# A gated attention and feed-forward block on one core: another order of its engines, and loads issued from ScalarE

## The chip, the cores and the metric

One Trainium2 chip, one of its cores. The metric is the device time of one execution in microseconds (us), lower is better. TensorE (PE) multiplies, VectorE (DVE), ScalarE (ACT) and GpSimd (POOL) compute elementwise, SyncE (SP) issues DMAs. TensorE's clock has two levels, 1.2 and 2.4 GHz; the profile gives the granted share of full speed.

## The reference

For 32 x 256 tokens of D = 256 features. The attention's mask lets each query see one key with the same position (and there are as many queries as keys), so attention is a projection by the value and output weights; its gate is tanh(g_x). Then a quantised feed-forward part with H = 1024:

```python
x = x + tanh(g_xattn[0]) * (context @ Wv @ Wout + bout)
h = layernorm(layernorm(x), ln1_g, ln1_b)
h = bitlinear(h, w1, b1)
h = gelu(h)
h = layernorm(h, ln2_g, ln2_b)
x = x + tanh(g_ffn[0]) * bitlinear(h, w2, b2)
```

where `bitlinear` rounds a token's features to 8 bits by its largest magnitude, and the weights to -1, 0, 1 by their mean magnitude, multiplies, and scales back.

## The kernel before

The 8192 tokens are cut into S = 16 sets of 128 partitions x T = 4 tiles. Each engine has a program of its own, written as `body(i)` for i from -3 to S + 1, and waits for the others on semaphores; the order of work is the order in which the bodies are written. A body deals with several sets at once:

- TensorE (L934): transposes the context of set i + 3 and 4 (`turn_context`, L937, into `bank_q`), multiplies by the joint weight `wvo` (`attention`, L1017), turns the rows of split statistics (`turn_rows`, L1053), adds bias and mean terms with small matmuls (`correction`, L1065, for y of set i - 1; `shift_first`, L1075, for h1 of set i + 1), makes the hidden layer of set i (`hidden`, L1084, alternately in `slot_a` and `slot_b`) and the second product of sets i - 2 (tiles 0, 1) and i - 3 (tiles 2, 3) (`second_product`, L1104, `second_bias`, L1115).
- ScalarE: quantises h1 of set i to `q1` (L540), copies contexts (L510) and rows (L556), quantises y of set i - 2 to `q2` (L549), and for each of the four tiles of set i a gelu (L566) and a square for the variance (L576).
- VectorE: residual and statistics of set i + 2, for set i - 1 four times `row` (y plus correction, L771) and `row_max` (L778), h1's shift and maximum (L757, L765), final results (`final`, L815), and the small operations of `scales` (L783) that give the quantisers' factors for set i + 1 (first layer) and i - 1 (second layer).
- POOL: gains (`gain`, L391, 128x1024 each; `gain_first`, L382), mean and variance (`norm_first`, L398, `variance`, L408), `root` (L373, a power of -0.5 for the two layers at once), `deviations` (L417) and five steps of `split` (L424), which cut six statistics into three bf16 parts for the rows.
- SP: loads x and context, issues DMA transposes of q1 and q2 (`turn_first`, L229; `turn_second`, L239) and stores. It issues in order: what stands behind a waiting load waits too.

Ahead of the bodies the kernel multiplies Wv by Wout (`turn_values`, `combine`), and quantises w1 and w2 in the first bodies. Bodies S and S + 1 finish the last sets.

```python
            for i in range(2, S):
                if live(i - 3):
                    turn_second(i - 3, 3)
                if live(i):
                    turn_first(i)
                if live(i - 2):
                    turn_second(i - 2, 0)
                if live(i + 4):
                    load_x(i + 4)
```

## Time and profile before

| what | value |
|---|---|
| median of 3 runs | 356.12 us (355.98 to 356.35) |
| profiled execution, its time | 356.32 us |
| its span, first to last instruction | 354.5 us |
| busy PE, DVE, ACT, POOL | 296.9, 294.9, 277.2, 265.2 us |
| mean granted TensorE clock | 0.957 |
| HBM traffic | 21.79 MB read, 8.41 MB written |

Busy time counts what an engine computes, not its semaphore or DMA instructions. A timeline row gives start, duration, engine, source line and tiles; the bracket at its end is idle time before it and what ended that. A name such as `q` or `rows` leaves out buffer numbers, so `q` is q1 at L544 and q2 at L553.

### The profile page before, as it was taken

The numbers are of one execution on the slowest core, as the hardware profiler recorded it, in microseconds if no ns is written. First come the engines' busy times: TensorE is split into PE (matmuls) and PEld (weight loads), VectorE is DVE, ScalarE is ACT, GpSimd is POOL, SyncE is SP. The second block draws the span as 40 slices with busy tenths as digits, with TensorE's granted clock in tenths as the row PEclk, the third lists the DMA queues.
The fourth block names the chain that finished last, engine by engine and source line by source line (L and its number), as shares of the span: only waits on it lengthen the run. The fifth ranks groups of instructions, "written<-read, shape, count | busy, mean of one in ns | idle before, by whom it ended". The sixth has DMA issues, their size and how long they took to land. (4 is left out here: it accounts for less than half of the span.)

```text
span 354.5 us, 5862 instructions
## 1 busy us (share of the span) xinstructions
PE 296.9 (84%) x1680; PEld 191.7 (54%) x1704; DVE 294.9 (83%) x521; ACT 277.2 (78%) x444; POOL 265.2 (75%) x298
## 2 busy tenths in 40 slices
PE   5998887889898979898989899989998849394566
PEld 4867463537475646465656565655655424242344
DVE  0268898989999999999999999989999948666582
ACT  2155696898989899998989898989898977779340
POOL 4045789997989888989898989898898986738410
PEclk9999999989999999999999999999999978978598
DMA  7956513364858685768666767595555445361457
GB/s 220 324 188 252 151 61 89 118 150 119 189 131 182 111 204 138 170 157 145 182 154 159 160 164 152 165 150 150 112 97 106 104 95 114 74 133 38 82 115 213
DMA packets 98634, 51.57 MB, mean 145 GB/s; under 512 B 87097, under 2 KB 89588, under 8 KB 98602
## 3 DMA queue, kind: packets, MB, share of 16 engines
q1 hardware_dynamic: 97706, 51.15, 59.5%
q8 instruction: 14, 0.23, 0.3%
q10 hardware_dynamic: 896, 0.04, 0.2%
q14 instruction: 18, 0.15, 0.1%
HBM read 21.79 MB, written 8.41 MB: 85 GB/s over the span
## 5 line engine op out<-in xcount | busy, mean ns | idle before, releaser
L395 POOL TENSOR_TENSOR y<-u,g_bc 128x1024 f32<-128x1024 f32 x64 | 151.0, 2368 | 15.3 <-ACT u L572 14.3
L776 DVE TENSOR_TENSOR y<-y,slot_c 128x1024 f32<-128x1024 f32 x64 | 77.7, 1214 | 23.3 <-PE slot_c L1070 23.3
L780 DVE TENSOR_REDUCE amax<-y 128x1 f32<-128x1024 f32 x64 | 78.0, 1218 | 1.8
L553 ACT ACTIVATE q<-y,scale 128x1024 f16<-128x1024 f32 x64 | 70.0, 1144 | 8.2 <-DVE scale L811 8.2
L580 ACT ACTIVATE junk<-u,usum 128x1024 bf16<-128x1024 f32 x64 | 73.7, 1151 | 2.0
L1112 PE MATMUL bank_f<-w2T,q2T 128*128 128x256 f16 x448 | 60.7, 281 | 7.4 <-DVE res L823 5.5
L1112 PEld LDWEIGHTS bank_f<-w2T,q2T 128*128 128x128 f16 x448 | 44.6, 101 | 23.5 <-DVE res L823 6.1
L1028 PE MATMUL slot_a<-wvo,ctxT 128*128 128x256 f32 x208 | 53.4, 386 | 1.0 <-ACT ctxT L515 1.0
L1070 PE MATMUL slot_c<-ln_rows,rows 128*128 128x512 bf16 x119 | 38.1, 397 | 16.6 <-ACT rows L563 7.2
L572 ACT ACTIVATE u<-slot_a,d 128x1024 f32<-128x1024 f32 x32 | 35.5, 1109 | 10.8 <-PE slot_a L1099 9.3
L1028 PEld LDWEIGHTS slot_a<-wvo,ctxT 128*128 128x128 f32 x208 | 36.3, 190 | 11.1 <-ACT ctxT L515 3.6
L1099 PE MATMUL slot_a<-w1T,q1T 128*128 128x512 f16 x128 | 40.5, 400 | 0.5 <-issue 0.2
L544 ACT ACTIVATE q<-h,scale 128x256 f16<-128x256 f32 x64 | 27.4, 500 | 13.8 <-DVE scale L811 13.8
L1099 PE MATMUL slot_b<-w1T,q1T 128*128 128x512 f16 x128 | 38.1, 380 | 0.0
L386 POOL TENSOR_TENSOR h<-x,g_bc 128x1024 f32<-128x1024 f32 x15 | 35.5, 2368 | 0.0
L572 ACT ACTIVATE u<-slot_b,d 128x1024 f32<-128x1024 f32 x32 | 35.1, 1097 | 0.0
L378 POOL TENSOR_TENSOR rstd<-var,half_neg 128x8 f32<-128x8 f32 x18 | 30.2, 1675 | 2.4
L1070 PEld LDWEIGHTS slot_c<-ln_rows,rows 128*128 128x128 bf16 x128 | 10.3, 99 | 33.9 <-issue 17.3
L823 DVE SCALAR_TENSOR_TENSOR res<-bank_f,d,x 128x256 f32<-128x256 f32 x56 | 24.4, 478 | 3.4 <-PE bank_f L1118 3.4
L745 DVE BATCH_NORM_STATS2 bn<-x 128x6 f32<-128x256 f32 x64 | 24.1, 418 | 1.0
L1096 PE MATMUL slot_b<-b_rows,rows 128*128 128x512 bf16 x64 | 24.5, 383 | 0.0
L515 ACT COPY ctxT<-bank_q 128x512 f32<-128x512 f32 x32 | 18.3, 572 | 6.2 <-PE bank_q L948 6.2
(136 smaller groups left out, 430.9 us busy)
## 6 DMA issues: line engine op xcount, KB each, us to landing
c_in<-in_ctx SPq DMA_DIRECT2D x16, 512.0 KB, 4.2
x_in<-in_x SPq DMA_DIRECT2D x16, 512.0 KB, 4.1
out<-res SPq DMA_DIRECT2D x31, 256.0 KB, 2.5
y<-in_L_ffn_w SPq DMA_DIRECT2D x2, 1024.0 KB, 9.0
u<-in_L_xattn_Wkv SPq DMA_DIRECT2D x2, 512.0 KB, 6.2
u<-in_L_xattn_Wout SPq DMA_DIRECT2D x2, 512.0 KB, 7.4
q2T<-q SPq DMA_TRANSPOSE x64, 3.3
g_bc<-in_L_ffn_ln_g SPq DMA_DIRECT2D x1, 512.0 KB, 5.5
```

The lines of the kernel that those rows point to most:

```text
L378: nc.gpsimd.tensor_tensor(rstd[:, j % 2, :, :], var[:, :, :], half_neg[:, :, :], ALU.pow) \
L386: nc.gpsimd.tensor_tensor(h1[:, :, :], x1[:, k % SETS, :, :], g1_bc[:, :].unsqueeze(1).to_broadcast([P, T, D]), ALU.mult) \
L395: nc.gpsimd.tensor_tensor(y[:, k % 3, t, :], u[:, t, :], g2_bc[:, :], ALU.mult).then_inc(gain2_done, 1)
L553: nc.scalar.activation(q2[:, t, :], y[:, k % 3, t, :], ACT.Copy, scale=scale[:, (k + 1) % 2, 1, t:t + 1]).then_inc(q2_done, 1)
L572: nc.scalar.activation(u[:, t, :], (slot_a, slot_b)[t % 2][:, :], ACT.Gelu, scale=d12[:, (i - 1) % 3, 0, t:t + 1], accum_out=usum[:, t:t + ...
L580: nc.scalar.activation(junk[:, t % 2, :], u[:, t, :], ACT.Square, scale=-float(H), bias=usum[:, t:t + 1], accum_out=usq[:, t:t + 1]) \
L776: nc.vector.tensor_tensor(line, line, slot_c[:, :], ALU.add).then_inc(y_done, 1)
L780: nc.vector.tensor_reduce(amax[:, 1, t:t + 1], y[:, k % 3, t, :], AX.X, ALU.max, apply_absolute_value=True).then_inc(amax2_done, 1)
L1028: nc.tensor.matmul(acc, ctxT[:, b * P:(b + 1) * P], wvo[:, j, :], start=(j == 0), stop=False)
L1070: terms = nc.tensor.matmul(slot_c[:, 512 * n:512 * (n + 1)], rows[:, (k + 1) % 2, t // 2, :], ln2_rows[:, t % 2, 512 * n:512 * (n + 1)], s ...
L1099: product = nc.tensor.matmul(slot[:, half], q1T[:, t * KD + k, :], w1T[:, k, half], start=False, stop=(k == KD - 1))
L1112: nc.tensor.matmul(product_bank(k, t), q2T[:, t, j, :], w2T[:, j, :], start=(j == 0), stop=False)
```

## The change

It rewrites the order on every engine and a few operations:

- From body 2 on the loads of x (set i + 4) and context (set i + 5) are issued by ScalarE, behind the second square and behind the fourth gelu; SP has only transposes and stores in its loop. SP's earlier loads are reordered.
- POOL's root is split: `root_first` (128x4) right after `norm_first`, `root_second` (128x4) where `root` stood; `variance` computes the mean row before it waits for the squares.
- `scales` has five operations instead of six (the lower limit joins others), `scale_weights` fewer, and `deq_inv` is gone.
- TensorE's body turns context earlier and makes second product 0 after the hidden layer, product 1 ahead of both attention halves. For bodies 13 to 15 `keep_warm` adds ten 128x512 matmuls of no use at the end, for 14 and 15 eight ahead of `turn_rows`.
- The end has one more body. POOL handles the last set's statistics in two pairs of tiles (`pair_root`, `pair_deviations`, a smaller `split` at i == S), and rows are turned three times.
- At the start the value weights come and are turned in four parts, with VectorE and ScalarE copying in turn; TensorE has 22 instead of 14 warm-up matmuls that wait for a memset of VectorE only; weight sums, clamps, copies and the first context turns change places.

```diff
@@ @block.sync: weight loads in four parts, order of the first loads, loads out of the loop @@
-            for n in range(2):
-                cols = slice(512 * n, 512 * (n + 1))
+            for n in range(4):
+                cols = slice(256 * n, 256 * (n + 1))
...
             for i in range(2, S):
                 if live(i - 3):
                     turn_second(i - 3, 3)
                 if live(i):
                     turn_first(i)
+                if live(i - 3):
+                    store(i - 3, 1)
                 if live(i - 2):
                     turn_second(i - 2, 0)
-                if live(i + 4):
-                    load_x(i + 4)
-                if live(i - 2):
                     turn_second(i - 2, 1)
-                if live(i - 3):
-                    store(i - 3, 1)
-                if live(i + 5):
-                    load_context(i + 5)
                 if live(i - 2):
                     turn_second(i - 2, 2)
...
@@ @block.gpsimd: the root in two parts, tiles 0 and 1 of the last set ahead @@
-                def root(j):
+                def root_first(k):
 
-                    wait(pool, var1_done, min(j + 2, S))
+                    wait(pool, var1_done, k + 1)
+                    wait(pool, scales_ready, scales_after(k - 3))
+                    nc.gpsimd.tensor_tensor(rstd[:, (k - 1) % 2, 0, :], var[:, 0, :],
+                                            half_neg[:, 0, :], ALU.pow).then_inc(root1_done, 1)
+
+                def root_second(j):
+
                     wait(pool, var2_done, j)
                     wait(pool, scales_ready, scales_after(j - 2))
-                    nc.gpsimd.tensor_tensor(rstd[:, j % 2, :, :], var[:, :, :], half_neg[:, :, :],
-                                            ALU.pow) \
+                    nc.gpsimd.tensor_tensor(rstd[:, j % 2, 1, :], var[:, 1, :], half_neg[:, 1, :],
+                                            ALU.pow).then_inc(rstd_done, 1)
...
                 def variance(k):
 
+                    wait(pool, gelu_done, T * k + T)
+                    wait(pool, split_steps, split_count(i))
+                    nc.gpsimd.tensor_scalar(stat[:, 2, :], usum[:, :], -1.0 / H, None, ALU.mult)
                     wait(pool, square_done, T * k + T)
                     wait(pool, std_done, i + 2)
-                    wait(pool, split_steps, split_count(i))
-                    nc.gpsimd.tensor_scalar(stat[:, 2, :], usum[:, :], -1.0 / H, None, ALU.mult)
...
+                if i == S - 1:
+                    gain(S - 2, 3)
+                    gain(S - 1, 0)
+                    gain(S - 1, 1)
+                    pair_root(0)
+                    return
+                if i == S:
+                    pair_root(1)
+                    return
+                if i == S + 1:
+                    gain(S - 1, 2)
+                    gain(S - 1, 3)
+                    return
...
@@ @block.scalar: body(i) @@
                     square(0)
                     gelu(1)
                     square(1)
+                if live(i + 4) and i > 1:
+                    load_x(i + 4)
+                if live(i):
                     gelu(2)
                     square(2)
                     gelu(3)
+                if live(i + 5) and i > 1:
+                    load_context(i + 5)
+                if live(i):
                     square(3)
...
@@ @block.vector: scales @@
-                    nc.vector.tensor_tensor(amax_g[one], amax[one], power, ALU.mult) \
-                        .then_inc(scale_steps, 1)
+                    nc.vector.scalar_tensor_tensor(
+                        out=amax_g[one], in0=amax[one], scalar=1.0 / STEP, in1=power,
+                        op0=ALU.mult, op1=ALU.mult).then_inc(scale_steps, 1)
                     wait(dve, scale_steps, base + 1)
-                    nc.vector.tensor_scalar(amax_g[one], amax_g[one], QEPS, None, ALU.max) \
-                        .then_inc(scale_steps, 1)
-                    wait(dve, scale_steps, base + 2)
                     nc.vector.reciprocal(amax_inv[one], amax_g[one]).then_inc(scale_steps, 1)
...
@@ @block.tensor: warm-up, dummies, order of a body @@
-            for n in range(14):
-                nc.tensor.matmul(slot_c[:, 0:T * ROWS], ones_b[:, :], zeros, start=True, stop=True)
...
+            pe.wait_ge(zeros_ready, 1)
+            for n in range(22):
+                nc.tensor.matmul(slot_c[:, 0:D], junk[:, 0, 0:P], junk[:, 0, P:P + D],
+                                 start=True, stop=True)
+            pe.wait_ge(consts, 13)
...
+                def keep_warm(n, first=False):
+
+                    wait(pe, gelu_done, T * (i - 1) + 3 if first else T * min(i, S - 1) + 3)
+                    for _ in range(n):
+                        nc.tensor.matmul(slot_a[:, 512:1024], ident_b[:, :], b1_rows[:, 0, 0:512],
+                                         start=True, stop=True)
...
                 if i == S:
+                    second_product(S - 3, 2)
                     turn_rows()
+                    second_bias(S - 3, 2)
                     correction(S - 1, 0)
                     correction(S - 1, 1)
...
                 if i == S + 1:
                     turn_rows()
+                    correction(S - 1, 2)
+                    correction(S - 1, 3)
...
+                if i > S - 3:
+                    keep_warm(8, True)
                 if i <= S + 1:
                     turn_rows()
...
                 if live(i + 3):
                     attention(i + 3, 1)
+                else:
+                    keep_warm(10)
```

TensorE in a middle set, behind the hidden layer's last tile, before (L948 turns context, L1080 shifts h1, L1028 and L1032 are attention, L1112 and L1118 the second product):

```order
L948 MATMUL bank_q<-ident_f,c_in 128x128 x4
L1080 MATMUL slot_c<-ln1_rows,rows 128x512 x2
L1028 MATMUL slot_a<-wvo,ctxT 128x256 x2
L1032 MATMUL slot_a<-bout_rows,ones_b 128x256
L1028 MATMUL slot_a<-wvo,ctxT 128x256 x2
L1032 MATMUL slot_a<-bout_rows,ones_b 128x256
L1112 MATMUL bank_f<-w2T,q2T 128x256 x8
L1118 MATMUL bank_f<-b2_rows,rows 128x256
```

and after the change (L1039 turns context, L1178 shifts h1, L1123 and L1127 are attention, L1213 and L1220 the second product):

```order
L1213 MATMUL bank_f<-w2T,q2T 128x256 x8
L1220 MATMUL bank_f<-b2_rows,rows 128x256
L1178 MATMUL slot_c<-ln1_rows,rows 128x512 x2
L1213 MATMUL bank_f<-w2T,q2T 128x256 x8
L1220 MATMUL bank_f<-b2_rows,rows 128x256
L1123 MATMUL slot_a<-wvo,ctxT 128x256 x2
L1127 MATMUL slot_a<-bout_rows,ones_b 128x256
```

The second context turn went from here to a place ahead of hidden tile 2, in exchange for second product 0, and product 1 moved ahead of attention.

ScalarE in a middle set, gelus and squares, before:

```order
L572 ACTIVATE u,usum<-slot_b,d12 128x1024
L580 ACTIVATE junk,usq<-u,usum 128x1024
L572 ACTIVATE u,usum<-slot_a,d12 128x1024
L580 ACTIVATE junk,usq<-u,usum 128x1024
L572 ACTIVATE u,usum<-slot_b,d12 128x1024
L580 ACTIVATE junk,usq<-u,usum 128x1024
L515 COPY ctxT<-bank_q 128x512
```

and after the change:

```order
L644 ACTIVATE u,usum<-slot_b,d12 128x1024
L652 ACTIVATE junk,usq<-u,usum 128x1024
L608 DMA x_in<-in_x 128x1024
L644 ACTIVATE u,usum<-slot_a,d12 128x1024
L652 ACTIVATE junk,usq<-u,usum 128x1024
L644 ACTIVATE u,usum<-slot_b,d12 128x1024
L603 DMA c_in<-in_ctx_1024 128x1024
L652 ACTIVATE junk,usq<-u,usum 128x1024
L577 COPY ctxT<-bank_q 128x512
```

Two DMA issues now stand between the activations.

POOL at the end, from the gains of the last set, before:

```order
L395 TENSOR_TENSOR y<-u,g2_bc 128x1024 x4
L413 TENSOR_SCALAR stat<-usum 128x4
L414 TENSOR_SCALAR var<-usq 128x4
L378 TENSOR_TENSOR rstd<-var,half_neg 128x8
L421 TENSOR_TENSOR stat<-var,rstd 128x2x4
```

and after the change:

```order
L428 TENSOR_TENSOR y<-u,g2_bc 128x1024 x3
L399 TENSOR_SCALAR stat<-usum 128x2
L400 TENSOR_SCALAR var<-usq 128x2
L404 TENSOR_TENSOR rstd<-var,half_neg 128x2
L412 TENSOR_TENSOR stat<-var,rstd 128x2
L474 CAST parts<-stat 128x2x2x3
```

Tiles 0 and 1 get their statistics and root behind the second gain of the last set; gains 2 and 3 stand behind the second pair.

## Rows read from the trace of the kernel before

**Rows 1.** Busy by stage: start:end, us, PE, PEld, DVE, ACT, POOL busy, PEclk, DMA, GB/s

```profile
0.00:57.56 57.56, 46.94 (x253) 34.65 (x256) 35.04 (x81) 27.12 (x45) 30.94 (x59) 1.00 0.61 198
57.56:274.81 217.25, 197.76 (x1145) 127.35 (x1163) 206.93 (x357) 198.71 (x323) 190.20 (x193) 0.99 0.64 146
274.81:295.34 20.53, 14.52 (x72) 7.51 (x72) 14.91 (x21) 15.83 (x27) 16.59 (x17) 0.83 0.53 118
295.34:315.72 20.38, 14.61 (x71) 7.54 (x72) 14.21 (x20) 15.72 (x26) 13.03 (x13) 0.83 0.42 92
315.72:354.50 38.78, 23.11 (x143) 14.65 (x142) 23.84 (x44) 19.80 (x27) 14.41 (x18) 0.82 0.47 111
```

**Rows 2.** ScalarE timeline, middle set: start us, us, engine line, op, tiles, [idle before]

```profile
163.12 3.23 ACT L553 ACTIVATE q<-y,scale 128x1024 f16<-128x1024 f32 x3
166.28 1.12 ACT L572 ACTIVATE u<-slot_a,d 128x1024 f32<-128x1024 f32 x1
...
171.23 1.12 ACT L572 ACTIVATE u<-slot_a,d 128x1024 f32<-128x1024 f32 x1
...
176.00 0.57 ACT L515 COPY ctxT<-bank_q 128x512 f32<-128x512 f32 x1
...
178.47 1.71 ACT L544 ACTIVATE q<-h,scale 128x256 f16<-128x256 f32 x4 [0.86 <-DVE scale L811]
```

**Rows 3.** VectorE timeline, w1's sum in the head, then a middle set

```profile
17.57 2.29 DVE L681 TENSOR_REDUCE wsum<-y 128x1 f32<-128x2048 f32 x1 [5.31 <-DMA y<-in_L_ffn_w]
...
163.92 1.22 DVE L776 TENSOR_TENSOR y<-y,slot_c 128x1024 f32<-128x1024 f32 x1 [0.21 <-PE slot_c L1070]
...
166.97 1.21 DVE L776 TENSOR_TENSOR y<-y,slot_c 128x1024 f32<-128x1024 f32 x1
...
176.76 0.88 DVE L823 SCALAR_TENSOR_TENSOR res<-bank_f,d,x 128x256 f32<-128x256 f32 x2 [0.18 <-PE bank_f L1118]
...
177.74 0.17 DVE L797 TENSOR_SCALAR amax_g<-amax_g 128x8 f32<-128x8 f32 x1
...
181.94 1.22 DVE L776 TENSOR_TENSOR y<-y,slot_c 128x1024 f32<-128x1024 f32 x1 [0.21 <-PE slot_c L1070]
```

**Rows 4.** TensorE timeline, middle set, from correction 2 to the turn

```profile
168.33 0.59 PE L1070 MATMUL slot_c<-ln_rows,rows 128*128 128x512 bf16 x2 [0.36 <-DVE y L776]
168.76 1.04 PE L1112 MATMUL bank_f<-w2T,q2T 128*128 128x256 f16 x8
...
179.10 1.04 PE L1112 MATMUL bank_f<-w2T,q2T 128*128 128x256 f16 x8
...
180.55 0.28 PE L1059 MATMUL slot_c<-ident_b,parts 128*128 128x128 bf16 x2 [0.30 <-POOL parts L437]
```

**Rows 5.** POOL timeline behind the last square, middle set

```profile
176.17 0.22 POOL L413 TENSOR_SCALAR stat<-usum 128x4 f32<-128x4 f32 x1 [1.21 <-ACT junk L580]
...
176.79 1.67 POOL L378 TENSOR_TENSOR rstd<-var,half_neg 128x8 f32<-128x8 f32 x1
178.53 0.20 POOL L421 TENSOR_TENSOR stat<-var,rstd 128x8 f32<-128x8 f32 x1
```

**Rows 6.** Loads by source line, ns min/median/max; then landing of q2T's transposes

```profile
L222 SPq DMA_DIRECT2D c_in<-in_ctx x16: 328/335/812, 3.6 to 227.5; - x16
...
L227 SPq DMA_DIRECT2D x_in<-in_x x16: 327/570/1224, 4.0 to 238.1; - x16
...
DMA to landing us min/median/max: 3.0/3.3/6.1
```

**Rows 7.** TensorE timeline, sets 14 and 15: turns, corrections, the last products

```profile
289.10 0.39 PE L1059 MATMUL slot_c<-ident_b,parts 128*128 128x128 bf16 x2 [1.96 <-POOL parts L437]
289.96 1.03 PE L1070 MATMUL slot_c<-ln_rows,rows 128*128 128x512 bf16 x2 [0.47 <-ACT rows L563]
...
329.77 0.40 PE L1059 MATMUL slot_c<-ident_b,parts 128*128 128x128 bf16 x2 [6.67 <-POOL parts L437]
...
345.40 1.14 PE L1112 MATMUL slot_a<-w2T,q2T 128*128 128x256 f16 x8 [3.32 <-DMA q2T<-q]
```

More of the change, by code:

```diff
@@ L781, in row_max, with scales @@
                                             apply_absolute_value=True).then_inc(amax2_done, 1)
-                def scales(kinds=slice(0, 2), those=slice(0, T)):
+                def scales(kinds=slice(0, 2), those=slice(0, T), turn=0):
                     shape = [P, kinds.stop - kinds.start, those.stop - those.start]
-                    base = 3 * (i + 1 + (those.start > 0))
+                    base = 2 * (i + 1 + turn)
                     one = (slice(None), kinds, those)
@@ L791, in scales @@
                     wait(dve, amax2_done, T * (i - 1) + those.stop)
-                    wait(dve, rstd_done, i + 2)
-                    wait(dve, split_steps, split_count(i))
-                    nc.vector.tensor_tensor(amax_g[one], amax[one], power, ALU.mult) \
-                        .then_inc(scale_steps, 1)
+                    wait(dve, root1_done, min(i + 2, S))
+                    wait(dve, rstd_done, i + (those.stop > 2 and i == S))
+                    wait(dve, split_steps, split_count(i + (i == S)))
@@ L815, in final @@
+                    nc.vector.scalar_tensor_tensor(
+                        out=scale[:, i % 2, kinds, those], in0=amax_inv[one], scalar=STEP / QEPS, in1=power,
+                        op0=ALU.min, op1=ALU.mult).then_inc(scales_ready, 1)
                 def final(k, t):
-                    if k == S - 1:
-                        wait(dve, ffn_done, T * k + (t + 1 if t > 1 else 2))
+                    if k == S - 2:
+                        wait(dve, ffn_done, T * k + T)
+                    elif k == S - 1:
+                        wait(dve, ffn_done, T * k + t + 1)
@@ L915, in body @@
                     row_max(i - 1, 3)
-                if i == S:
-                    scales(slice(1, 2), slice(2, 4))
                 if live(i + 1):
```

344 lines of the change are left out of this document (205 added, 139 removed).

## The prediction, made before the changed kernel ran

> **What bounds the kernel now.** I cut the span at the first gelu of sets 0+1, 13, 14 and 15 and read each stretch in the busy times by stage [rows 1]. Sets 1 to 13 take 217.25 us for 12 periods, 18.10 each; VectorE is busy 206.93 of it, ScalarE 198.71, TensorE 197.76, POOL 190.20. Nothing idles for long, so a ring of engines sets the pace. Sets 13 and 14, with less work on TensorE and VectorE, take 20.53 and 20.38, and the last stretch 38.78; there TensorE's granted clock is 0.83, 0.83 and 0.82, so part of each runs at 1.2 GHz instead of 2.4.
>
> The timelines of one middle set show the ring. ScalarE starts q1 at 178.47 after waiting 0.86 for VectorE's scales [rows 2]. VectorE starts the first y row of a set at 163.92 and again at 181.94, a period of 18.02, after waiting only 0.21 for TensorE [rows 3]. TensorE waits 0.36 for y before a correction and 0.30 for POOL before it turns the rows [rows 4]. POOL waits 1.21 for the last square, then runs statistics, a `pow` of 1.67, deviations and five split steps [rows 5]. The ring is: scales at 160.4 (a period before 178.47), ScalarE to the end of the last square at 176.0, POOL to 180.55, turn, copy and correction to 181.94, VectorE until its scales at 196.45 (a period after 178.4). That is 36.0 for two periods, almost without slack: 18.0.
>
> **The change in the middle sets.** (a) POOL behind the square: one 0.22 statistic with its gap moves ahead of the wait (-0.29), and `pow` is made for 4 elements there, the other 4 earlier in the set. No row shows a `pow` of 4: it lies between the 0.20 of a plain 8-element operation and the 1.67 of 8 [rows 5]. I take the middle, 0.93, since an 8-element `pow` costs so much more than plain work on 8 that it seems to go with elements. Chain -0.29 -0.74 = -1.03. POOL's own work becomes at most 18.02 -1.21 -1.67 +2x0.93 +0.1 (a gap) = 17.1: not a bound.
> (b) Scales: five operations instead of six; the removed one lasts 0.17, 0.20 with its gap. VectorE also waits 0.18 for the second product, which now comes earlier. Its own work is 18.02 -0.21 -0.18 -0.20 = 17.43 [rows 3].
> (c) TensorE's order: nothing is added or lost in a middle set. From the first y row to the end of the second: 166.97 + 1.21 - 163.92 = 4.26 [rows 3]. From there to correction 2, 0.15; from 168.33 through the unchanged quantity of work to the turn, less its wait (180.55 - 0.30), 11.92; turn, copy, correction and hand-over to VectorE, 180.55 to 181.94, 1.39 [rows 3, 4]. Sum 17.72. **This one-period ring, VectorE to TensorE and back, is what is late next.** The ring (a) falls from 36.0 by 1.03, 0.38 and 0.18 (gelus 0 and 1 with squares take 171.23 - 166.28 = 4.95, gelus 2 and 3 take 4.77: gelu 2 waits for its product [rows 2], which now comes before the second product) to 34.4, or 17.2 a period, below it.
> (d) Loads from ScalarE: 10 of x behind square 1 and 9 of context behind gelu 3. SP's issues of the same loads take 0.34 and 0.57 in the median, 0.81 and 1.22 at most [rows 6]. If ScalarE's queue runs ahead of its arithmetic they cost 0; if it stands still, 0.91 a set, at most 2.03. The nearest row is SP's and says nothing on overlap; I take 0, because both stand behind an activation of 1.1 us that is already running. The cover is exactly that activation. Queued behind are the remaining gelus, the copy of ctxT and the attention that needs it. That ring is ScalarE q2 3.23, four gelus and squares 9.54, copy 0.57 [rows 2], TensorE's last transposes, attention and product until its turn 3.65 (from 176.6, where the copy ends, to 180.25, the same work in either order), turn and copy of rows 0.6: 17.6. It has 0.1 to spare; whatever issue costs beyond that lengthens each of 10 periods. On SP, where a load now waits for nobody, transposes are never queued behind a load's wait, which removes part of the occasional long period. They need 3.0 to 6.1 to land (median 3.3) [rows 6]. The loads have a whole period to land.
> The middle thus goes from 217.25 to 12 x 17.72 = 212.6: **-4.6**.
> The DMA side has a contrary rule. Trainium skill, DMA: Bandwidth & Descriptors, "Issuing engines are not separate DMA queues": requests from any engine run on the same 16 DMA engines, and another issuer saves only its sequencer's time. By it transposes meet the same traffic and about two periods could stay 0.5 longer, 1.0 more in all; the landing spread fits it, but no row has loads from ScalarE.
>
> **Head.** Weights come in halves, VectorE joins in the copies, warm-up starts without POOL, but w1 still arrives at 17.57 [rows 3]. Attention 0 may be 1.0 to 2 earlier but VectorE first sums w1 for 2.29, so what remains is about 0.7: the weights' sum no longer stands in front of hidden 0. The shortened POOL chain then meets set 1, limited by the copies of ctxT. I take **-1.2** for everything up to set 1's gelu at 57.56; between 0 and -2.3.
>
> **Sets 14 and 15.** Now TensorE turns at 289.10 after waiting 1.96 for POOL, the two corrections behind it last 1.03 against 0.59 in the middle, and the next gelu starts at 295.34 [rows 1, 4, 7]. Dummy matmuls (`keep_warm`) fill the waits: 10 at the end of a set, 8 before the turn. At 0.43 for two 128x512 [rows 4] they last 2.15 and 1.72. Counted from a set's first gelu, final results let the product end at 12.2, eight dummies end at 13.95, POOL would be ready at 13.05, so the turn is 0.9 late for them; then rows, three q2 of 1.08 and gelu at 17.85. Two sets: 35.7 against 40.91, **-5.2**. ScalarE is the end there, so TensorE's speed alone buys nothing more.
>
> **Tail.** Root, split and turn for tiles 0 and 1 of set 15 go ahead of its last gelus. Before, the turn came 329.77 - 315.72 = 14.05 behind the first gelu. Now POOL has those rows at about 9.2, but TensorE still has both products, ten dummies and one more product, to 11.2: the turn is 2.9 earlier, the first y row 3.3 earlier. The second half turns at 16.5, behind y row 1. Two more y rows with maxima, scales at 24.85, five splits, the third turn at 26.8 where the last four products began at 29.68 (345.40) [rows 7]. They still start cold after a 4 us gap, as they do now after 3.32. Their cost of about 5.4, and a last transpose that lands at 30.4, put the end at 35.4 in place of 38.78: **-3.4**.
>
> **Sum.** 354.5 -1.2 -4.6 -5.2 -3.4 = 340.1 span. The profiled execution took 356.32, 1.82 more than its span, and lies 0.2 above the median of 356.12. 340.1 + 1.82 - 0.2 = **341.7 us**.
>
> **Rivals.**
> A, `pow` has a fixed price, near 1.67 for 4 elements. For: every one of the 18 rows has 8 elements. Then POOL carries up to 15.2 + 3.34 = 18.5 a period, and 12 x 0.8 = 9, with 2 more in the last sets: 353. Decides from about 1.3 upwards. Against: plain POOL work scales. Chance 0.10.
> B, ScalarE stands still for SP's median times, 0.91 a set: 0.8 x 10 = 8: 349.7. Chance 0.14.
> C, dummies do not hold the clock. Eight then last 3.4, the turn is at 15.6, and correction, product and hidden run at 1.2 GHz: 21.8 a set instead of 17.85, +8: 349.7. For: TensorE is mostly idle there. Chance 0.08. Trainium skill, TensorE: Matmul & The Clock Gate, "What's actually happening": the array is throttled by default and activity releases it, which gives 341.7 if the dummies count and 349.7 if they do not. The granted clocks of rows 1 agree with the first half; no row here has dummies between waits.
> D, **slower**: the loads stop ScalarE for their long times, 0.81 + 1.22 = 2.03 a set. 17.6 + 2.03 = 19.6 against 17.72, +19 over ten periods: 360.7. Slower begins at about 1.6 a set. For: SP's own rows reach it. Against: medians are under half. Chance 0.03.
> E, the change does more: TensorE's gaps close until VectorE's 17.43 is the bound, and the tail's products stay warm: -3.5 and -1.5: 336.7. Chance 0.10.
> The forecast itself, 339 to 345: 0.55.
>
> **How the numbers follow.** 336.5 to 350 takes in the forecast, B, C and E and leaves out A, D and their combinations. A measurement tells 0.2% from nothing, 0.7 us. Only D and combinations of A, B and C reach 355.4: faster 0.95, same 0.02, slower 0.03.
>
> **What would show it.** Right: q1 to q1 at 17.7 in the middle with a VectorE wait of about 0.3 for TensorE at the first y row; `pow` near 0.9; no gap ahead of gelu 2; 17.9 between gelus 13, 14 and 15 at clock above 0.95; first y row of set 15 12.7 behind its first gelu. Wrong: periods of 18.4 with POOL never waiting for the square (A), gaps of 0.3 to 1.2 behind the loads on ScalarE (B, D), corrections of 1.03 in sets 14 and 15 (C).

## The result, and the profile after

The changed kernel takes 344.59 us (median of 4 executions, 343.29 to 346.18) beside 356.24 (355.98 to 356.75) for the kernel before on the same chip: ratio 0.967, 95% interval 0.963 to 0.972. 341.7 was forecast, with 336.5 to 350. The profiled execution took 343.99 us, with a span of 342.0. Three executions among the experiments below were slow ones (e5's profiled one with 778.87 us, one of e6 with 452.92, one of e9 with 346.75): the ratios leave them out, the medians of the table don't. The busy times and the clock of the profiled execution:

```profile
PE 299.9 (88%) x1735; PEld 192.6 (56%) x1760; DVE 292.4 (86%) x501; ACT 276.0 (81%) x446; POOL 269.3 (79%) x322
...
PEclk9999999999999999999999999999999999999989
```

Busy by stage, cut at the same gelus as [rows 1]: start:end, us, PE, PEld, DVE, ACT, POOL busy, PEclk, DMA, GB/s:

```profile
0.00:54.44 54.44, 47.99 (x261) 35.41 (x264) 34.78 (x78) 27.13 (x47) 29.97 (x61) 1.00 0.61 204
54.44:271.85 217.41, 195.94 (x1144) 125.32 (x1162) 205.55 (x344) 197.53 (x322) 195.12 (x206) 1.00 0.62 146
271.85:289.37 17.52, 15.88 (x90) 8.53 (x91) 13.78 (x20) 15.59 (x25) 15.29 (x16) 1.00 0.49 106
289.37:307.06 17.69, 15.95 (x91) 8.42 (x91) 13.94 (x20) 15.58 (x27) 13.10 (x14) 1.00 0.56 105
307.06:342.00 34.94, 24.13 (x154) 14.97 (x154) 24.39 (x43) 20.13 (x29) 15.80 (x27) 0.93 0.65 144
```

Against [rows 1]: head -3.12, sets 1 to 13 **+0.16**, the next two sets -5.70, the end -3.84; together -12.50. All of the gain is at the two ends of the kernel. In the middle nothing is left of the 4.6 us forecast.

Yet the middle does have the period that was forecast. VectorE's first y rows of sets 8 and 9:

```profile
178.24 1.22 DVE L860 TENSOR_TENSOR y<-y,slot_c 128x1024 f32<-128x1024 f32 x1 [0.21 <-PE slot_c L1167]
...
195.85 1.22 DVE L860 TENSOR_TENSOR y<-y,slot_c 128x1024 f32<-128x1024 f32 x1 [0.21 <-PE slot_c L1167]
```

That is 17.61, of which 0.21 is a wait: VectorE is full with 17.40 of work. In [rows 3] the period of 18.02 held waits of 0.21 and 0.18 and no other idle time, so VectorE had 17.63 of work and was as full as this in the kernel before. But from first gelu to first gelu the 12 periods are 17.93, 17.24, 17.91, **19.63**, 17.95, 17.96, 17.51, 17.61, **19.15**, 18.07, 17.98 and 18.47. TensorE's waits from 60 to 270 us name what fills the long ones (line and tile that waited, releaser: us in total, times, longest):

```profile
PE bank_f L1213 <- DMA q2T<-q: 5.7, 8, 2.0
```

In the kernel before, the same wait has two rows of 1.6 and 1.4 us. The worst place, in the period of 19.63: TensorE's second product of tile 1 waits, and the attention behind it is late for VectorE.

```profile
117.14 1.03 PE L1213 MATMUL bank_f<-w2T,q2T 128*128 128x256 f16 x8 [1.95 <-DMA q2T<-q]
```

```profile
118.32 0.88 DVE L909 SCALAR_TENSOR_TENSOR res<-bank_f,d,x 128x256 f32<-128x256 f32 x2 [0.55 <-PE bank_f L1220]
120.27 0.75 DVE L818 SCALAR_TENSOR_TENSOR x<-slot_a,tg,x_in 128x512 f32<-128x512 f32 x1 [0.48 <-PE slot_a L1127]
122.66 0.75 DVE L818 SCALAR_TENSOR_TENSOR x<-slot_a,tg,x_in 128x512 f32<-128x512 f32 x1 [0.85 <-PE slot_a L1127]
```

SP's queue at that place (L254 is the store, L248 the transpose of q2), then the loads from ScalarE's queue in the same microseconds:

```profile
108.26 0.33 SPq L254 DMA_DIRECT2D out<-res  x1
108.70 4.60 SPq L248 DMA_TRANSPOSE q2T<-q  x3
```

```profile
111.14 0.33 ACTq L608 DMA_DIRECT2D x_in<-in_x  x1
...
113.82 0.34 ACTq L603 DMA_DIRECT2D c_in<-in_ctx  x1
```

ScalarE had finished q2 of tile 0 by about 105.3 (its three q2 start at 104.09 and end at 107.32), but SP passes the store at 108.6, since that store waits for the fourth final result. Then three transposes go out back to back, and 1 MB of loads joins them. Two things are thus to be suspected: the loads, and that store.

In the last sets TensorE's dummies (L1228), turn and correction, where [rows 7] had a wait of 1.96 and a correction of 1.03:

```profile
283.93 1.89 PE L1228 MATMUL slot_a<-b_rows,ident_b 128*128 128x512 bf16 x8
285.66 0.28 PE L1155 MATMUL slot_c<-ident_b,parts 128*128 128x128 bf16 x2
286.40 0.61 PE L1167 MATMUL slot_c<-ln_rows,rows 128*128 128x512 bf16 x2 [0.46 <-ACT rows L635]
...
333.57 0.28 PE L1155 MATMUL slot_c<-ident_b,parts 128*128 128x128 bf16 x2 [0.84 <-POOL parts L474]
```

### The profile page after: what moved, and what is told of

It reads as the page before. It is cut to its first block, busy times and chain, and to the rows that moved or that the text cites. A ratio compares the mean times of both kernels' runs of the same rounds, so it can differ in the third digit from the quotient of the medians.

```text
span 342.0 us, 6023 instructions
## 1 busy us (share of the span) xinstructions
PE 299.9 (88%) x1735; PEld 192.6 (56%) x1760; DVE 292.4 (86%) x501; ACT 276.0 (81%) x446; POOL 269.3 (79%) x322
## 4 chain that ended last, share of the span: by engine, by line
DVE 29%; PE 22%; issue 14%; DMA 13%; ACT 4%; POOL 2%; SPq 2%; DVEq 0%; ACTq 0%; POOLq 0%
DVE y L860 14%; DMA q2T<-q 13%; DVE amax L864 7%; PE bank_f L1213 6%; PE slot_a L1123 5%; DVE res L909 5%; DVE h L845 3%; PE slot_c L1167 2%; PE slot_a L1228 2%; ACT u L644 1%; PE bank_q L1039 1%; ACT q L625 1%; ACT rows L635 1%; SPq L254 1%; PE slot_b L1197 1%
## 5 line engine op out<-in xcount | busy, mean ns | idle before, releaser
L1213 PE MATMUL bank_f<-w2T,q2T 128*128 128x256 f16 x456 | 59.0, 273 | 6.2 <-DMA q2T<-q 5.7
L1213 PEld LDWEIGHTS bank_f<-w2T,q2T 128*128 128x128 f16 x456 | 43.7, 98 | 24.7 <-issue 11.0
L1167 PE MATMUL slot_c<-ln_rows,rows 128*128 128x512 bf16 x119 | 36.3, 380 | 21.3 <-DVE y L860 10.6
L1123 PE MATMUL slot_a<-wvo,ctxT 128*128 128x256 f32 x208 | 52.2, 381 | 1.0 <-ACT ctxT L577 1.0
L1123 PEld LDWEIGHTS slot_a<-wvo,ctxT 128*128 128x128 f32 x208 | 35.5, 190 | 7.6 <-ACT ctxT L577 1.5
L1197 PE MATMUL slot_a<-w1T,q1T 128*128 128x512 f16 x128 | 38.1, 379 | 0.3
L616 ACT ACTIVATE q<-h,scale 128x256 f16<-128x256 f32 x64 | 27.4, 497 | 12.7 <-DVE scale L895 12.7
L1167 PEld LDWEIGHTS slot_c<-ln_rows,rows 128*128 128x128 bf16 x128 | 8.8, 97 | 41.1 <-issue 27.3
L909 DVE SCALAR_TENSOR_TENSOR res<-bank_f,d,x 128x256 f32<-128x256 f32 x57 | 25.9, 477 | 3.5 <-PE bank_f L1220 3.2
L577 ACT COPY ctxT<-bank_q 128x512 f32<-128x512 f32 x32 | 18.2, 569 | 7.1 <-PE bank_q L1039 7.1
L1194 PE MATMUL slot_b<-b_rows,rows 128*128 128x512 bf16 x63 | 23.8, 379 | 0.0
L818 DVE SCALAR_TENSOR_TENSOR x<-slot_a,tg,x_in 128x512 f32<-128x512 f32 x26 | 19.4, 747 | 4.1 <-PE slot_a L1127 4.1
```

The costliest lines, as they stand in the source:

```text
L909: nc.vector.scalar_tensor_tensor(out=res[:, k % 2, t, :], in0=product_bank(k, t), scalar=d12[:, (k + 1) % 3, 1, t:t + 1], in1=x1[:, k % SE ...
L1123: nc.tensor.matmul(acc, ctxT[:, b * P:(b + 1) * P], wvo[:, j, :], start=(j == 0), stop=False)
L1167: terms = nc.tensor.matmul(slot_c[:, 512 * n:512 * (n + 1)], rows[:, (k + 1 + late) % 2, t // 2, :], ln2_rows[:, t % 2, 512 * n:512 * (n + ...
L1197: product = nc.tensor.matmul(slot[:, half], q1T[:, t * KD + k, :], w1T[:, k, half], start=False, stop=(k == KD - 1))
L1213: nc.tensor.matmul(product_bank(k, t), q2T[:, t, j, :], w2T[:, j, :], start=(j == 0), stop=False)
```

## The experiments

Twelve kernels ran, each beside the kernel before on the same chip. "Middle" is the time from the first gelu of set 1 to that of set 13 in the profiled execution; "period n" and "set n" below stand for the stretch that ends with the first gelu of set n. Each middle is of one execution; two pairs of kernels have the same code in their bodies there, and differ by 0.34 us (the change and e4) and 0.30 (e6 and e9).

| run | what it is | median us | ratio to before, 95% | middle |
|---|---|---|---|---|
| the change | | 344.59 | 0.967 (0.963 to 0.972) | 217.41 |
| e1 | loads on SP again | 343.28 | 0.961 (0.955 to 0.966) | 216.89 |
| e2 | both loads late, ScalarE | 340.81 | 0.955 (0.949 to 0.960) | 214.09 |
| e3 | no loads | 341.36 | 0.955 (0.950 to 0.960) | 214.84 |
| e4 | no dummies | 346.51 | 0.969 (0.964 to 0.974) | 217.75 |
| e5 | before, loads on ScalarE | 355.87 | 0.999 (0.997 to 1.002) | |
| e6 | second store back | 339.97 | 0.957 (0.953 to 0.961) | 213.68 |
| e7 | both stores last | 338.49 | 0.951 (0.948 to 0.953) | 211.18 |
| e8 | e7 and late loads | 338.34 | 0.951 (0.948 to 0.954) | 211.67 |
| e9 | e6, code shifted | 343.37 | 0.962 (0.956 to 0.967) | 213.98 |
| e10 | e7, loads on SP | 338.17 | 0.949 (0.945 to 0.953) | 211.92 |
| e11 | e7, whole `pow` | 337.95 | 0.948 (0.944 to 0.953) | 211.05 |
| e12 | e7, TensorE's old order | 339.20 | 0.952 (0.947 to 0.957) | 212.92 |

### Who issues the loads, where, and whether there are any (e1, e2, e3, e5)

e1, both loads back on SP:

```diff
                     turn_second(i - 2, 0)
+                if live(i + 4):
+                    load_x(i + 4)
+                if live(i - 2):
                     turn_second(i - 2, 1)
+                if live(i + 5):
+                    load_context(i + 5)
```

> The changed kernel, with both loads issued by SP again, at the places they had before (x of set i+4 between the transposes of q2 tiles 0 and 1, context of set i+5 behind the store). Theory A (the periods of 17.9 to 19.6 us in the middle come from loads that ScalarE issues close together, beside the transposes of q2 that the earlier second products wait for): on SP the two loads are spread again, sets 1 to 13 take 212 to 215 us where the changed kernel took 217.41, TensorE's waits for transposed q2 fall from 5.7 us to under 3, time 340 to 342. Rival B (the long periods come from the order of TensorE and of SP's transposes and store, whoever issues the loads): middle 217 to 219, waits for transposed q2 of 5 us or more, time 344 to 347. Rival C (moving the loads was the gain, SP's queue being blocked by waiting loads): slower than the changed kernel, 347 or more, with SP waiting for VectorE's residual ahead of a transpose.

Measured: 343.28 us, middle 216.89, with periods up to 18.99. Theory A and rival C fall: spread out on SP, the loads do no less harm, and taking them off SP was no gain. Rival B's middle of 217 to 219 comes nearest, though the waits for q2T fell to 4.2 us where it had 5 or more, and the time lies just below its 344 to 347.

e2, x load moved behind the fourth gelu:

```diff
-                if live(i + 4) and i > 1:
-                    load_x(i + 4)
...
                     gelu(3)
+                if live(i + 4) and i > 1:
+                    load_x(i + 4)
                 if live(i + 5) and i > 1:
                     load_context(i + 5)
```

> The changed kernel, with both loads still issued by ScalarE, but x of set i+4 moved from behind the second square to behind the fourth gelu, next to the context. Theory A (the two loads beside the transposes of q2 tiles 0 and 1 make these land late): if it is the x load that meets them, the waits for transposed q2 fall to under 3 us and sets 1 to 13 take 212 to 214 us, time 339 to 342; if two loads at once are worse than two apart, waits grow to 8 us or more, middle 219, time 346. Rival B (order alone, whatever the loads do): nothing changes, middle 217, waits 5 to 6 us, time 343.3 to 346.

Measured: 340.81 us, the wait for q2T down from 5.7 to 2.4, no period of 19 us:

```profile
54.33:268.42 214.09, 196.46 (x1144) 126.09 (x1162) 205.04 (x344) 197.45 (x322) 194.85 (x205) 0.99 0.61 148
```

So the x load does meet the transposes. Half of the loss is gone, not all.

e3 drops the `load_x` and `load_context` calls of ScalarE's body and caps the waits for them.

> The changed kernel without the loads of x from set 6 on and of context from set 7 on: those sets compute on the data that are still in the buffers, so these two inputs' traffic (1 MB a set) is left out and all arithmetic stays. Theory A (transposes late because of the loads' traffic): every q2 transpose lands in 3.0 to 3.6 us from set 6 on, TensorE's waits for them vanish, periods of 17.5, sets 1 to 13 in 211 to 213.5 us, time 338 to 341. Rival B (order alone): the waits for transposed q2 stay at 4 us or more, middle 216 to 218, time 343 to 345. Rival D (no wait, the engines' own rings are simply 17.9 a period): waits fall but periods stay 17.9, time 343 or more.

Measured: 341.36 us, middle 214.84: between theory A and rival B, and no better than e2. Theory A's waits didn't vanish (4.0 us in all for q2T from 60 to 270 us), and q2 transposes took up to 4.9 us to land, not 3.6. Here the transposes go out as late as before, yet tile 1 comes in time: SP's rows, and TensorE's product of tile 1, which starts without a wait where it lost 1.95:

```profile
108.34 0.34 SPq L254 DMA_DIRECT2D out<-res  x1
108.78 4.44 SPq L248 DMA_TRANSPOSE q2T<-q  x3
```

```profile
115.14 1.04 PE L1209 MATMUL bank_f<-w2T,q2T 128*128 128x256 f16 x8
```

The loads' traffic is needed for the two long periods. But periods of 18.2 to 18.3 remain in sets without any load, so there is a second cause.

e5 makes the loads' move alone in the kernel before (the same two `if` blocks in ScalarE's body, the same two calls taken out of SP's loop).

> The kernel before with one part of the change alone: from body 2 on the loads of x (behind the second square) and of context (behind the fourth gelu) are issued by ScalarE. Theory A (issuing from ScalarE costs its arithmetic nothing, and TensorE's order of before hides transposes that land late): within 1 us of the kernel before, spacing of the gelus unchanged at 2.38 us. Rival (the loads' move was itself a gain, SP being freed): 2 to 5 us faster than before. Rival (moved loads make the transposes of q2 tiles 1 and 2 late here too): 2 to 5 us slower.

Measured: 355.87 us, the same as before within 0.35%, which is 1.2 us. There is no trace of an ordinary execution of e5, so the gelus' spacing is read in the changed kernel: the load at 111.14 above lies beside a square that runs from 111.13 to 112.28, and the next gelu starts at 112.28. **By itself, the move from SP to ScalarE neither gains nor costs anything that these runs can tell from nothing.**

### The stores in SP's queue (e6, e7, e8, e10)

e6, the second store of set i-3 where it stood before the change:

```diff
-                if live(i - 3):
-                    store(i - 3, 1)
                 if live(i - 2):
                     turn_second(i - 2, 0)
                     turn_second(i - 2, 1)
+                if live(i - 3):
+                    store(i - 3, 1)
```

> The changed kernel with one SP instruction moved: the second store of set i-3, which waits for VectorE's fourth final result, goes behind the transposes of q2 tiles 0 and 1, as before the change, in place of ahead of them. Theory G (gate: q2 tile 0 is ready 2 to 3 us before SP gets past that store, so three transposes start late and are issued back to back, and tile 1 is late for its earlier product): the waits of 1 to 2 us for q2 tile 1 go, no period of 19 us or more, sets 1 to 13 take 213 to 215 us instead of 217.41, time 339.5 to 342. Rival L (the loads alone make those transposes late): long waits remain, middle 216 to 218, time 343 to 346.

Measured: 339.97 us, no period above 18.27:

```profile
54.38:268.06 213.68, 197.61 (x1161) 125.52 (x1162) 204.97 (x344) 197.54 (x322) 194.89 (x206) 1.00 0.60 149
```

Theory G holds, with the loads left where they are: **one store moved ahead of three transposes cost 3.7 us of the middle.** The long periods need both, the late start (e6 removes it) and the x load beside them (e2 and e3 remove that).

These two don't yet say why only periods 5 and 10 are long. In every period from 4 to 12 of the changed kernel the three transposes start 1.2 to 1.3 us behind the first gelu, and the x load follows 3.6 us behind it. Yet tile 1 lands 3.4 to 3.8 us after its issue in seven of these periods, and 6.5 and 6.4 us after it in periods 5 and 10. What those two have besides is an instruction packet in the middle of the three transposes, that is a packet of one of the two queues that the profile lists with the kind "instruction": q14 at 111.2 us, q8 at 202.3. The instruction queue in the window of the three transposes, and their median us to landing, first in period 5 (108.70 to 113.30), then in period 10 with SP's row (199.44 to 204.46), last in period 7 (146.26 to 150.50), which has no such packet:

```profile
q14 instruction: 1, 0.01, 0.6%
...
q2T<-q SPq DMA_TRANSPOSE x3, 5.8
```

```profile
199.44 5.02 SPq L248 DMA_TRANSPOSE q2T<-q  x3
```

```profile
q8 instruction: 1, 0.02, 1.2%
...
q2T<-q SPq DMA_TRANSPOSE x3, 5.5
```

```profile
q2T<-q SPq DMA_TRANSPOSE x3, 3.6
```

Two more traces agree. e4, below, has the same code up to set 12: its q14 packet falls in the same place in period 5 (21.74 us; TensorE's wait of 2.39 is followed by 3.4 us at half clock), but none falls while the three transposes of period 10 are issued (the next comes at 206.5), and that period takes 17.61:

```profile
202.16 4.13 SPq L248 DMA_TRANSPOSE q2T<-q  x3
```

e3 has both packets and no loads: tile 1 lands in 3.3 and 4.9 us, and the periods take 17.52 and 17.74. So a long period had three things at once: transposes that start late, the x load, and an instruction packet between them. That rests on where the packets fall in these traces; no run moved one of these packets alone.

e7, both stores behind all transposes of the body:

```diff
                     turn_second(i - 2, 2)
-                if live(i - 2):
-                    store(i - 2, 0)
+                if live(i - 3):
+                    store(i - 3, 0)
+                    store(i - 3, 1)
```

> The changed kernel with both stores of set i-3 behind all three transposes of q2 of set i-2, so that no transpose is issued behind a store any more (the first store comes some 8 us later than in the changed kernel, the loads stay where they are). Theory S (besides the gate, the store right ahead of the transpose of q2 tile 3 stretches that transpose's issue from 1.29 to between 1.4 and 2.4 us, and the period by as much): every issue of tile 3 takes 1.23 to 1.3 us, periods of 17.5 to 17.6 throughout, sets 1 to 13 in 211 to 213 us, time 337.5 to 340. Rival R (the issue is stretched by something else, such as the transposes of q1 or instruction loading): issues of 1.8 to 2.4 us stay, middle 214 to 216, time 340.5 to 343.

Measured: 338.49 us. From period 4 to period 12 every one is 17.61 or 17.62, and from 60 to 270 us no wait of TensorE for q2T is left:

```profile
54.80:265.98 211.18, 196.69 (x1162) 125.96 (x1163) 204.48 (x344) 196.89 (x323) 194.22 (x205) 1.00 0.60 149
```

The middle and the time are theory S's, its cause is not. SP's rows of set 6, the transpose of tile 3, then of tiles 0 to 2, then the stores:

```profile
136.37 2.04 SPq L248 DMA_TRANSPOSE q2T<-q  x1
...
141.12 4.02 SPq L248 DMA_TRANSPOSE q2T<-q  x3
...
145.19 1.05 SPq L254 DMA_DIRECT2D out<-res  x2
```

With no store ahead of it, tile 3's issue still takes 2.04 here. It starts about 0.4 earlier (11.1 behind the first gelu of the set before, not 11.5 to 11.6), and it lands 3.3 us after its start, where the one of set 6 in e6, behind a store and issued in 2.13, took 4.1. That covers the stretch. What stretches it is still open here: rival R.

e8 puts e2's edit on top of e7, and e10 gives e7's loads back to SP, behind the stores.

> The changed kernel with both stores behind the three transposes of q2 and the load of x moved behind the fourth gelu, next to that of context. Theory A+S (three causes, each a transfer beside or ahead of a transpose; with all of them out of the way VectorE's own work of 17.5 a period is the bound): 211 to 212.5 us for sets 1 to 13, no wait for transposed q2 above 0.3, time 337 to 339. Rival R (stretched issues have another cause): as fast as the late loads alone, 340 to 342. Rival T (both stores and both loads then fall in the same 4 us, and the loads reach into the next transpose of tile 3): issues of tile 3 of 1.6 us or more, time 341 or more.

Measured: 338.34, middle 211.67. Nothing beyond e7: once transposes start in time, the x load's place no longer matters. (The expected "no wait above 0.3" held too. Rival T's sign, issues of tile 3 of 1.6 or more, showed up to 2.05, but its time did not.)

> The kernel with both stores behind the three transposes of q2, and both loads issued by SP again, behind those stores, in place of ScalarE. Theory (what counts is what stands ahead of a transpose in SP's queue; behind the last transpose a load may stand on SP as well as on ScalarE): periods 17.6, sets 1 to 13 in 211 to 212.5 us, time within 1 us of 338.5. Rival (SP waits for VectorE's residual or TensorE's context turn with the load and reaches the next transpose late, or the loads' issue from ScalarE is worth something by itself): 2 us or more slower.

Measured: 338.17 us, middle 211.92: the theory. A third comparison of ScalarE with SP as issuer, and again no difference.

### What stretches the issue of tile 3 (e9)

The edit on e6, at TensorE's start:

```diff
+            for n in range(64):
+                nc.tensor.matmul(slot_c[:, 0:16], junk[:, 0, 0:P], junk[:, 0, P:P + 16],
+                                 start=True, stop=True)
             pe.wait_ge(consts, 13)
```

> The kernel with the second store behind two transposes, with 64 more warm-up matmuls of 16 columns at TensorE's start, of no use to the output: TensorE's program becomes 128 instructions longer ahead of everything else, about half of one packet of the instruction queue q8 (14 packets, 0.23 MB in all). Theory I (the issue of the transpose of q2 tile 3 is stretched from 1.29 us to between 1.6 and 2.4 in just those sets where a q8 packet of instructions is being fetched beside it: sets 4, 6, 7, 12 and 13 without the shift): the fetches come some 10 us earlier, so other sets are hit; sets 6, 7 and 13 return to 1.29 and 17.6 us, and each issue above 1.5 again has a q8 packet within 3 us of it, and no other has. Rival P (the stretch belongs to these sets for another reason, such as DMA of data or the age of a buffer): 6, 7 and 13 stay at 2.1 us. Time within 2 us of 340, the head perhaps 1 us longer.

SP's rows of e6, tile 3 in sets 6 and 8, and the instruction queue q8 (packets, MB, share of the 16 engines), which has a packet in the window from 135.73 to 138.73 and none from 172.17 to 175.17:

```profile
136.73 2.13 SPq L248 DMA_TRANSPOSE q2T<-q  x1
...
173.17 1.29 SPq L248 DMA_TRANSPOSE q2T<-q  x1
```

```profile
q8 instruction: 1, 0.02, 2.3%
```

The same for e9, with a q8 packet in the window from 173.68 to 176.68 and none from 138.45 to 141.45:

```profile
139.45 1.30 SPq L248 DMA_TRANSPOSE q2T<-q  x1
...
174.68 1.88 SPq L248 DMA_TRANSPOSE q2T<-q  x1
```

```profile
q8 instruction: 1, 0.02, 2.4%
```

In e9 the stretched sets are 3, 8, 9 and 10 (2.09, 1.88, 2.19, 2.00); 4, 6, 7, 12 and 13 are back at 1.29 or 1.30. Theory I holds, and the periods move with the issues: e6 has 18.03, 18.07, 18.27, 17.77 and 18.27 in periods 4, 6, 7, 12 and 13, 2.4 us above 17.61 in all, and e9 has 18.26, 18.06, 18.29 and 18.06 in 3, 8, 9 and 10. Over the 13 traces other than e5's, sets 3 to 13 in each, there are 143 issues of tile 3. In 56 of them a q8 packet started between 1 us ahead of the issue and 2 us behind its start: 54 took 1.40 to 2.44 us, two didn't (1.23 in e8, 1.28 in the kernel before). The 87 without such a packet took 1.40 or less. The time, 343.37, is above the 342 allowed: the head grew by 1.70 with the extra matmuls, and period 15 took 19.35 in place of 17.61, with a wait of 1.64 for q2T at 304.56 and a q8 packet between 300 and 303. That this packet caused that wait isn't shown by itself.

### The forecast's own terms (e4, e11, e12)

e4: `keep_warm` returns at once.

> The changed kernel without the dummy matmuls of the last sets (ten at the end of bodies 13 to 15, eight ahead of the turns in 14 and 15); nothing that the output needs is left out. Theory of the prediction (they hold TensorE's granted clock): sets 13 and 14 return from 17.6 to between 19.5 and 21.8 us, with corrections near 1.03 instead of 0.61 and a granted clock near 0.83, time 348 to 353. Rival (the shortened POOL chain alone gained in these sets): sets 13 and 14 stay at 17.5 to 18.3, time 342.5 to 345; without the dummies in front of it the turn could even come up to 0.9 earlier.

Stages of sets 13 and 14, and TensorE's correction in set 14:

```profile
272.21:292.22 20.01, 14.90 (x72) 7.59 (x72) 14.66 (x21) 15.69 (x25) 16.32 (x18) 0.83 0.42 93
292.22:310.78 18.56, 13.57 (x71) 7.20 (x72) 13.34 (x18) 15.69 (x25) 12.45 (x13) 0.91 0.45 100
```

```profile
286.67 1.04 PE L1167 MATMUL slot_c<-ln_rows,rows 128*128 128x512 bf16 x2 [0.46 <-ACT rows L635]
```

The clock is back at 0.83 and 0.91 and the correction at 1.04, as the prediction's theory had it, and the two sets take 38.57 in place of 35.21: 3.4 of the 5.7 us come from the dummies. Even with the clock down, 38.57 is 2.3 below the 40.91 of before. POOL's shorter chain, the shorter scales and TensorE's order are all in that rest, and no run separates them. The time, 346.51, is below the 348 to 353 expected: the second set ran at half clock only in part, and the end, 33.62, is 1.3 shorter than the change's. The Trainium skill, TensorE: Matmul & The Clock Gate, "What's actually happening", has activity release the throttle. These traces agree, and they show that matmuls of no use count as activity: granted clock 1.00 with them, 0.83 and 0.91 without.

e11, the second root of 4 elements is one of 8 again:

```diff
-                    root_first(i + 2)
...
+                        nc.gpsimd.tensor_tensor(rstd[:, j % 2, :, :], var[:, :, :], half_neg[:, :, :],
+                                                ALU.pow).then_inc(rstd_done, 1)
```

> The kernel with both stores behind the transposes, with the root undone in the middle: for bodies 1 to 13 one power of 8 elements a partition where the second one of 4 stood, as before the change. Theory of the prediction (POOL's chain is shared by two periods and has 0.4 to 0.8 us of slack a period): at most 0.2 us a period, 0 to 2.5 in all, time 338.5 to 341. Rival (square, root, scales, gelu form a ring of one period, without slack: 1.67 in place of 1.04 us goes straight onto it, less 0.1): 18.1 to 18.3 a period, 6 to 8 us in all, time 344.5 to 346.5.

```profile
54.72:265.77 211.05, 194.75 (x1145) 125.93 (x1163) 204.48 (x344) 196.93 (x323) 190.19 (x193) 1.00 0.60 149
```

```profile
187.77 1.67 POOL L392 TENSOR_TENSOR rstd<-var,half_neg 128x8 f32<-128x8 f32 x1
...
189.84 0.30 POOL L479 CAST parts<-stat 128x72 bf16<-128x72 f32 x1
```

Splitting the `pow` is worth nothing in the middle. With the split POOL waits 0.67 for VectorE's scales ahead of its first split step (e7); without it POOL arrives just in time (the row at 189.84 has no wait):

```profile
190.06 0.29 POOL L474 CAST parts<-stat 128x72 bf16<-128x72 f32 x1 [0.67 <-DVE scale L895]
```

e12 restores TensorE's order in the bodies (second product 0 between corrections 2 and 3).

> The kernel with both stores behind the transposes, with TensorE's order of before in the bodies (second product 0 between corrections 2 and 3, its context turn behind hidden 3, attention half 0 ahead of second product 1); the dummy matmuls stay. Theory of the prediction (gelu 2 then waits for its product, and the second half of a set is 0.18 to 0.4 us longer): 17.8 to 18.0 a period, 2 to 5 us in all, time 340.5 to 343.5. Rival (TensorE's order is worth nothing by itself, the rest of the ring hides it): 338 to 339.5.

```profile
54.22:267.14 212.92, 196.18 (x1145) 126.79 (x1163) 204.78 (x344) 198.03 (x323) 194.29 (x205) 1.00 0.60 148
```

Periods of 17.68 to 17.74 with one of 18.29, and 339.20 against 338.49 us with overlapping intervals: TensorE's order is worth about 0.1 in an undisturbed period. That is the rival's range of time, and less than half of what the theory gave. VectorE waits again for the second product, as in [rows 3], and no longer for the first y row:

```profile
206.82 0.88 DVE L909 SCALAR_TENSOR_TENSOR res<-bank_f,d,x 128x256 f32<-128x256 f32 x2 [0.18 <-PE bank_f L1220]
```

## Why the prediction was right, and which step of it was not

The time lies in the range and on the forecast's side, and the median is 2.9 above the forecast. The number is better than the mechanism behind it. The middle, a third of the forecast gain, gave nothing, and the two ends and the last sets gave 2.9 more than forecast; that these partly cancel is luck. The profiled execution's terms:

- **Head, -1.2 forecast, -3.12 measured.** Two terms were too small. "w1 still arrives at 17.57": it is summed 0.87 earlier. "What remains is about 0.7" up to the first gelu: the first rows are copied at 28.02, where the row of before stood at 30.19, and the first gelu starts at 37.80 for 40.28, 2.48 earlier. From there to set 1's gelu another 0.64 is gained (16.64 for 17.28). Timeline of VectorE's sum, then ScalarE's rows and gelu:

```profile
16.70 2.29 DVE L771 TENSOR_REDUCE wsum<-y 128x1 f32<-128x2048 f32 x1 [6.25 <-DMA y<-in_L_ffn_w]
```

```profile
28.02 0.37 ACT L635 COPY rows<-slot_c 128x256 bf16<-128x256 bf16 x1 [2.40 <-PE slot_c L1155]
...
37.80 1.11 ACT L644 ACTIVATE u<-slot_a,d 128x1024 f32<-128x1024 f32 x1 [2.20 <-PE slot_a L1197]
```

- **Middle, -4.6 forecast, +0.16 measured: the step that failed.** Where nothing disturbs it a period is as forecast: 17.61 (17.72), VectorE's own work 17.40 (17.43), first y row waiting 0.21. But VectorE sets it, not a ring of engines. VectorE has no idle time in such a period except this 0.21, and before the change that and the 0.18 of [rows 3]. Of the 0.41 between 18.02 and 17.61, 0.20 is the operation taken out of `scales` with its gap, 0.18 is the wait for the second product that is gone, and 0.03 is left over. The failing sentence is "on SP, where a load now waits for nobody, transposes are never queued behind a load's wait". True of loads, but the diff also put a *store* that waits ahead of the transposes, and second product 1 now needs its transpose sooner. That move in SP's queue was never costed. Of the 6.2 us between 217.41 and e7's 211.18, 3.7 are that store, with the x load and an instruction packet beside the late transposes (e6), and 2.5 are the instruction packets that stretch tile 3's transpose just behind the other store (e7, e9). In the kernel before such a stretch exists too (1.82 at the transpose of set 6, period 18.23).
- **(a), POOL.** `pow` of 4 takes 1.04, forecast 0.93, between the plain 0.20 and 1.67:

```profile
181.88 1.04 POOL L383 TENSOR_TENSOR rstd<-var,half_neg 128x4 f32<-128x4 f32 x1
```

 Rival A is out (its 12 x 0.8 is 9.6, not 9, which changes nothing). But e11 shows that this gain of 0.63 was not what shortened the period.
- **(c), TensorE's order**, "nothing is added or lost": about 0.1 a period gained (e12).
- **(d), loads from ScalarE at nothing: right.** 0.33 each, beside an activation that is running; rivals B and D are out. On the DMA side the prediction's contrary rule was the better guide. The Trainium skill, DMA: Bandwidth & Descriptors, "Issuing engines are not separate DMA queues", has the DMAs of all issuers run on the same 16 DMA engines. These runs agree: who issues makes no difference beyond noise (e1, e5, e10), the traffic next to a transpose does (e2, e3). Transposes of q2 now take 3.1 to 6.5 us to land, median 3.5, where [rows 6] had 3.0 to 6.1 and 3.3; the 1.0 that the prediction worked out for two periods was too small: periods 5 and 10 are 3.6 above 17.61 in all.
- **Sets 13 and 14, -5.2 forecast, -5.7 measured**: 17.52 and 17.69 for 17.85, the correction 0.61. Rival C is out.
- **End, -3.4 forecast, -3.84 measured**: first y row 12.56 behind the first gelu (12.7), third turn 26.5 (26.8). The last four products, forecast to start cold (at half clock), ran at full clock, 1.03 or 1.04 each, as rival E had it.

The sum of the errors is -1.92 +4.76 -0.50 -0.44 = +1.90 in the profiled execution, its time outside the span is 0.17 more than before, and it lies 0.6 below the median instead of 0.2 above. Rival E is close to what the kernel would have been with its stores elsewhere (338.49 in e7, 336.7 forecast): VectorE is its bound in e7, with TensorE at full clock and 17.61 from y row to y row:

```profile
175.77 1.22 DVE L860 TENSOR_TENSOR y<-y,slot_c 128x1024 f32<-128x1024 f32 x1 [0.21 <-PE slot_c L1167]
...
193.38 1.22 DVE L860 TENSOR_TENSOR y<-y,slot_c 128x1024 f32<-128x1024 f32 x1 [0.21 <-PE slot_c L1167]
```

e7, e8, e10 and e11 (337.95 to 338.49 us) are 1.8% to 1.9% faster than the changed kernel, and can't be told apart.

What stays open: the shares of 0.20 and 0.18 in the shorter period are read from VectorE's rows. e12 brings the wait of 0.18 back and takes the 0.21 away, 0.1 in all; no run undoes the shorter `scales` or POOL's mean row alone. The share of each edit in the head's 3.1 us was not tried either.

## What to carry to other kernels

Read an in-order DMA queue as you read an engine: for each instruction that the diff moves in it, ask what it waits for and what stands behind it. Here a store that waits for a result, put ahead of transposes whose data were ready, cost 3.7 us, while the engine that issued the loads made no difference that could be measured. When one period is as forecast and the mean isn't, list the periods, and look for what only the long ones have: two long ones and several slightly long ones had different causes, and moving two stores in the queue ended both. And before you call a ring of engines the bound, add up one engine's idle time in an undisturbed period: VectorE had 0.39 of 18.02.

## What the runs showed of the hardware

- Fetches of program code get in the way of a kernel's own DMAs. The instruction queue q8 moves 14 packets, 0.23 MB, in this kernel, and a DMA transpose of one q2 tile issued beside one kept SP busy for 1.40 to 2.44 us in 54 of 56 cases, in place of 1.23 to 1.40. 128 more TensorE instructions at the start moved the packets, and with them the stretched transposes, from sets 4, 6, 7, 12 and 13 to 3, 8, 9 and 10 (e6, e9). So where the instruction packets fall can change which periods are long: 0.2 to 0.7 us each behind tile 3's transpose, 1.5 to 2.0 in periods 5 and 10 of the changed kernel.
- One transpose occupies SP for 1.23 to 1.30 us, longer than ScalarE takes for the tile (three q2 in 3.23): three issued back to back last 4.0 us in e7.
- GpSimd's `pow` grows with its elements: 0.72 us for 2 a partition, 1.04 for 4 and 1.67 for 8, beside 0.20 for a plain product of 8 [rows 5].
